# One selector per step: a single VectorE instruction behind each sum, in place of masks and selectors in batches of four

## The reference, cut to what matters

```
def _rel_graph_conv(h, src, dst, etypes, norm, basis, comp, bias, loop_w, apply_relu):   # L0, twice, 4 bases
    hb = jnp.einsum('nd,bdo->bno', h, basis)
    coef = comp[etypes]
    m = coef[:, 0, None] * hb[0][src]
    ...                                                      # the other bases
    m = m * norm[:, None]
    agg = jax.ops.segment_sum(m, dst, num_segments=n)
    out = agg + bias + h @ loop_w
...
    weight = jnp.einsum('rb,bio->rio', w_comp, bases)        # L1: 32 relations, 8 bases
    h_rel = jnp.einsum('ni,rio->rno', x, weight)
    out = jax.ops.segment_sum(h_rel[etype, src] * norm, dst, num_segments=n_nodes)
```

## Time and profile before

| | before |
|---|---|
| median of three runs | 3198.17 us |
| profiled execution | 3180.53 us, span 3179.2 us |
| busy: PE, DVE, ACT, POOL | 3042.3, 2097.8, 1382.1, 1161.1 us |
| L988, sums into G | x664, 454.8 us busy, 685 ns mean, idle before it 154.3 us |
| L864, products with the selector | x1328 matmuls, 659.7 us busy |
| stages with `aggregate` | L0a 42 to 350 us, L0b 532 to 795 us, L1 937 to 1232 us |

### The profile page before, as it was taken

How to read it: one execution, slowest core, us unless ns; L and a number is a source line. 1 busy time by engine, 2 the same in 40 slices (tenths; PEclk the granted TensorE clock), 3 DMA queues, 4 the chain that set the end, 5 groups by cost and what they waited for, 6 DMA issues and landing times.

```text
span 3179.2 us, 44609 instructions
## 1 busy us (share of the span) xinstructions
PE 3042.3 (96%) x14954; PEld 2194.2 (69%) x14954; DVE 2097.8 (66%) x4794; ACT 1382.1 (43%) x2130; POOL 1161.1 (37%) x938
## 2 busy tenths in 40 slices
PE   7999998999979999999999999999999999999999
PEld 3334676444753346876448998789988899879987
DVE  7999423787348864254367678667776777767777
ACT  7999632001340023342254555345543555435554
POOL 4555336556356643431204022511125111441023
PEclk9999998999989999999999999999999999999999
DMA  3555433556236643324103011220014001130012
GB/s 95 149 145 149 165 103 113 162 164 176 79 103 176 170 138 101 97 68 143 33 30 106 8 37 50 66 70 14 31 50 125 18 8 64 43 103 14 8 64 79
DMA packets 125748, 279.37 MB, mean 88 GB/s; under 512 B 22727, under 2 KB 40455, under 8 KB 124499
## 3 DMA queue, kind: packets, MB, share of 16 engines
q0 software_dynamic: 40320, 132.15, 14.8%
q1 hardware_dynamic: 83762, 141.72, 14.2%
q10 hardware_dynamic: 1440, 2.62, 0.2%
HBM read 227.83 MB, written 27.46 MB: 80 GB/s over the span
## 4 chain that ended last, share of the span: by engine, by line
PE 79%; DVE 12%; issue 3%; DMA 3%; ACT 2%; POOL 1%; DVEq 0%; SPq 0%; POOLq 0%; ACTq 0%
PE bank L152 15%; PE bank L154 15%; PE bank L153 15%; PE bank L864 13%; PE bank L2465 5%; PE bank L875 4%; DVE G L988 4%; PE bank L2129 3%; PE bank L1771 2%; PE bank L839 2%; DVE y_tile L2081 1%; DVE y_tile L2083 1%; DVE x_stats L2064 1%; PE bank L1047 1%; DMA yT_lo<-yT_new_lo 1%
## 5 line engine op out<-in xcount | busy, mean ns | idle before, releaser
L864 PE MATMUL bank<-gathered,selector 128*128 x1328 | 659.7, 612 | 52.5 <-SPq L827 30.2
L988 DVE TENSOR_TENSOR G<-G,bank 128x512 f32 x664 | 454.8, 685 | 154.3 <-PE bank L864 102.3
L864 PEld LDWEIGHTS bank<-gathered,selector 128*128 128x128 f32 x1328 | 219.2, 191 | 326.3 <-issue 301.4
L2553 ACT CAST probT<-bank 128x512 fp32r<-128x512 f32 (+2 forms) x480 | 212.1, 516 | 263.8 <-PE bank L2465 262.9
L2635 DVE CUSTOM_DVE_ANT_0 prob<-bank,count_by_src 128x512 f32<-128x512 f32 (+1 forms) x480 | 258.3, 588 | 60.4 <-PE bank L154 60.4
L849 ACT COPY G<-bank 128x512 f32<-128x512 f32 x160 | 81.2, 658 | 497.7 <-PE bank L839 497.7
L1445 POOL TENSOR_TENSOR weight_parts<-weight_ring,weight_parts 128x512 fp32r<-128x512 f32 x130 | 187.3, 1441 | 301.0 <-ACT weight_parts L1378 300.9
L891 ACT ACTIVATE sign_src<-node_iota_16bit,src_float 128x1251 bf16<-128x1251 f16 x208 | 278.6, 1341 | 41.6 <-PE bank L875 19.3
L1404 DVE TENSOR_TENSOR lhs_parts<-G,lhs_parts 128x640 fp32r<-128x640 f32 x122 | 101.5, 832 | 293.9 <-ACT lhs_parts L1376 293.7
L2561 DVE TENSOR_TENSOR probT<-bank,probT 128x512 fp32r<-128x512 f32 (+2 forms) x480 | 254.2, 585 | 51.0 <-ACT probT L2553 50.2
L152 PE MATMUL bank<-weight_parts,lhs_parts 128*128 128x512 f32 x680 | 268.0, 394 | 9.4 <-POOL weight_parts L1445 4.5
(11 more groups left out here) (293 smaller groups left out, 6935.2 us busy)
## 6 DMA issues: line engine op xcount, KB each, us to landing
weight_ring<-in_L_gnn_basis SPq DMA_DIRECT2D x64, 256.0 KB, 2.8
weight_ring<-in_L_gnn_bases SPq DMA_DIRECT2D x64, 256.0 KB, 2.7
x_L<-x_rows SPq DMA_DIRECT2D x50, 256.0 KB, 4.4
x_rows<-x_L SPq DMA_DIRECT2D x50, 256.0 KB, 5.7
yT_hi<-yT_new_hi SPq DMA_DIRECT2D x4, 2560.0 KB, 10.8
yT_lo<-yT_new_lo SPq DMA_DIRECT2D x4, 2560.0 KB
count_rows<-count SPq DMA_DIRECT2D x10, 640.0 KB, 5.9
count_by_dst<-count_rows SPq DMA_DIRECT2D x10, 640.0 KB, 8.3
```

Of the source, the lines that this page charges most:

```text
L864: pe.matmul(bank[s % banks][:], sel[:, s % SELECTORS, :], xs[:, ds(slot[s % BATCH], 1), :].rearrange("p t d -> p (t d)"), start=True, stop ...
L988: dve.tensor_tensor(g, g, bank[s % banks][:], ALU.add).then_inc(*added.inc())
L2553: ins = act.copy(hi, of)
```

## The change

In `aggregate`, the mask tile and the batches go. `select(s)` is one DVE instruction for one step (scalar_tensor_tensor, 128 x 128: grid equals the place, which is a column operand, times coefficient). Eight are made ahead of step 0; after that the selector of step s + 8 is issued right behind the sum of step s, ahead of whatever else that step has for DVE (a count, a one-hot tile, a guest). PE waits for one selector at each step instead of for a batch each four steps.

```
-SELECTORS = 3 * BATCH
+SELECTORS, AHEAD = 3 * BATCH, 2 * BATCH
...
         for s in range(steps):
+            pe.wait_ge(*selected(s + 1))
             if s % BATCH == 0:
                 slot, tiles = (table(C.tile_of_step[path][0:1, s // BATCH, w, :], PE, w, (RING - 1, T)[w])
                                for w in range(2))
-                pe.wait_ge(*selected(s // BATCH + 1))
...
-    def select(i):
-
-        first, n = i * BATCH, min(BATCH, steps - i * BATCH)
-        if first >= SELECTORS:
-            dve.wait_ge(*multiplied(first - SELECTORS + n))
-        if i:
-            dve.wait_ge(*selected(i))
-        dve.tensor_tensor(
-            same[:, 0:n, :],
-            grid.rearrange("p (t n) -> p t n", t=1).to_broadcast([P, n, path.nodes]),
-            C.place[path][:, first:first + n].rearrange("p (t n) -> p t n", n=1).to_broadcast([P, n, path.nodes]),
-            ALU.is_equal).then_inc(*compared.inc())
-        dve.wait_ge(*compared(i + 1))
-        at = first % SELECTORS
-        dve.tensor_tensor(
-            sel[:, at:at + n, :].rearrange("p t (b n) -> p t b n", b=nb),
-            same[:, 0:n, :].rearrange("p t (b n) -> p t b n", b=1).to_broadcast([P, n, nb, path.nodes]),
-            co[:, :, first:first + n].rearrange("p (b n) t -> p t b n", n=1).to_broadcast([P, n, nb, path.nodes]),
-            ALU.mult).then_inc(*selected.inc())
+    def select(s):
+
+        if s >= SELECTORS:
+            dve.wait_ge(*multiplied(s - SELECTORS + 1))
+        dve.scalar_tensor_tensor(
+            sel[:, s % SELECTORS, :].rearrange("p (b n) -> p b n", b=nb),
+            grid.rearrange("p (b n) -> p b n", b=1).to_broadcast([P, nb, path.nodes]), C.place[path][:, s:s + 1],
+            co[:, :, s:s + 1].to_broadcast([P, nb, path.nodes]), ALU.is_equal, ALU.mult).then_inc(*selected.inc())
...
-        select(0)
-        select(1)
+        for s in range(AHEAD):
+            select(s)
...
-                if s // BATCH + 2 < batches:
-                    select(s // BATCH + 2)
...
             dve.tensor_tensor(g, g, bank[s % banks][:], ALU.add).then_inc(*added.inc())
+            if s + AHEAD < steps:
+                select(s + AHEAD)
```

More of the change, by code:

```diff
@@ L332, in prepare @@
     C.after_G = M.at
-    M.at += 4 * (RING * D + SELECTORS * P + BATCH * PATH0.nodes)
+    M.at += 4 * (RING * D + SELECTORS * P)
     C.counting = CountBuffers(C)
@@ L766, in aggregate @@
     if counting:
-        grid, same = C.iota[:, 0:path.nodes], M.new("same_node", [P, BATCH, path.nodes])
+        grid = C.iota[:, 0:path.nodes]
     else:
         grid = bank[3][:, 0:path.nodes]
-        same = bank[3][:, P:P + BATCH * path.nodes].rearrange("p (t n) -> p t n", t=BATCH)
     gathered = [C.landed(f"gathered{u}") for u in range(RING)]
@@ L773, in aggregate @@
     place_free = C.event("gathered_free")
-    compared, selected = C.event("selector_compared"), C.event("selected")
+    selected = C.event("selected")
     added = C.event("added")
@@ L778, in aggregate @@
     turned, taken = C.event("G_turned"), C.event("G_taken")
-    batches = -(-steps // BATCH)
     per = P // path.nodes
```

## The result

The kernel after takes **3233.9 us** (median of 4 runs, 3230.7 to 3235.1), the kernel before 3199.0 (4 runs, 3192.6 to 3200.8): ratio 1.0111, interval 1.0098 to 1.0123, 35 us slower. The forecast was 3202, in a range of 3182 to 3226.

The account below looks back on a forecast made before the run. Waits were taken to decide: L0a's loop through DVE's count, sums in L1, PE and DVE alternating in L0b. +38 - 24 - 10.5 = +3.5, called +4, on 3198.2 gave 3202 us, range 3182 to 3226.

Parts of the forecast that it names:

- L0a, +38: L0a: three selectors per group of four steps stand inside the loop through DVE's third count, 49 groups: +38 us (29 to 50).
- L1, -24: L1, steps 3 to 179: selectors vanish in DVE's idle time between sums, 0.897 us a step instead of 1.04: -24 us.
- L0b, -10.5: L0b: no batch between sums, though guests find the idle time taken: -10.5 us (-4 to -14).
- PE (0.858) and POOL stay under that: L1: PE's step and POOL's gather (1.26 us against 1.32 a tile) fit the new pace; 1.5 us given back.
- Rival A: L0b and L1: gathers set the pace once a tile takes over 1.32 us, half of both gains lost: 3219 us; chance 0.15.
- Rival B: All three stages: small DVE instructions don't overlap, so L1 gains 2, L0b nothing, L0a pays 50: 3246 us; chance 0.06.
- Rival C: L0a: the loop doesn't close through the count, so the three selectors are free: -34.5, 3164 us; chance 0.13.
- The base: Whole kernel: the profiled 3180.5 us lies 0.55% under the runs' median; the same +4 us was carried over to 3198.2.

Follow-up runs that it names:

- the second profile: The kernel before, unchanged, profiled again on chip 7: 3200.5 us, where its first profiled execution took 3180.5.

## Why the prediction was wrong

- **L0a, +38:** right. Loop, place, price (0.26) and number of selectors held; a group took 6.58 for a forecast of 6.57, the stage grew by 41 us, and the term alone cost 40.8. Outside the loop the same instructions leave the kernel at the time of the one before (3205.5 beside 3205.8), with some 4 us left in the stage.
- **L1, -24, and L0b, -10.5:** the failed step is "PE (0.858) and POOL stay under that", for which I gave back 1.5 us. It looked at the work of both engines and put the wait for PE's counts at nothing. Pace and place held to the hundredth. But on chips with late counts (the runs of the result took as long as those do, and the kernel after has the same ten pauses again on chip 14) a pace under some 1.05 us a step isn't let through while POOL gathers: by the profiles 2.8 us in L1 and 3.3 in L0b came of 34.5, by the ratios above 3 to 4 together. 41 - 6 = 35, the measured loss.
- **What was right in it:** with no late counts (plain loads on both sides) the two terms come out at 28.1 and 10.5. The arithmetic of DVE stood; the wrong part was to take the waits that the earlier trace rows show as the only ones there are. Those rows could not show this one: they come from an execution in which no count is late. In the second profile, with late counts, the kernel before is at 187.7 / 176 = 1.07 a step, as the kernel after is (1.07), so the step's new price of 0.90 found nothing to gain.
- **Rival A** named the gathers and gave 3219. The bound is tied to them, but not as it said: hardly a tile was late, L862 waited for one for 0.3 us in 155 (the waits of L1), and POOL itself stood 35.5 us for counts of PE:

```profile
POOL gathered L792 <- PE bank L862: 35.5, 35, 2.6
...
DVE G L973 <- PE bank L862: 17.8, 20, 1.9
...
PE bank L862 <- SPq L825: 0.3, 1, 0.3
```

- **Rival B** is out: the selector starts 0.09 before the sum's row ends, the next instruction 0.08 to 0.09 before the selector's row ends, and with plain loads it vanishes in the gap (169 sums in 155 us). **Rival C** is out: L0a grew by the three selectors.
- **The base:** I saw that the profiled execution lay 18 us under the median and carried the difference over as a constant. It lay in L0b and L1, 10 and 8 us, the very stages whose slack I counted on. Its stages (265.2 and 287.3) are those of chip 3 (265.7 and 286.7), so the profile most likely came from a chip that shows no pauses, and the times from one that does.

What stays open is what makes a count late. Shown: the late counts of L0b and L1 go when plain loads of as many bytes stand in place of the gathers, on a chip that has them; they don't depend on bytes (half of each gather leaves eleven pauses) or on the number of selector counts, or much on PE's load; they differ between chips; and it is PE's counts that are held, several at once, not its multiplications and not DVE's counts. Not shown: which part of a gather does it, its indirect form, POOL's longer work for it or its scattered addresses, since the plain loads changed all three; and whether the recording itself has a part in it. Every time on record comes with a span and a granted clock of the same execution, so no run here shows the kernel unrecorded.

## What to carry to other kernels

Before a freed gap is booked as gain, ask what the profile can't show because the present bound hides it, and test that with an edit that removes the present bound cheaply. A timing from one chip need not hold on the next. When a profile's own time differs from the median, find the stage in which it differs first, for that stage's slack is what a forecast rests on. A small instruction is free or costs its full 0.26 us by its place in the loop that closes last; count the loop's instructions, not the engine's share.

## What the runs showed of the hardware

- The same kernel takes 3182 us on one chip and 3198 to 3206 on three others, and 17.6 of the 20 us between two profiles lie in L0b and L1. L0a gathers as well, a tile in some 1.8 us at its slower steps, and is as long on both kinds of chip (301.8 and 300.8 us).
- Late counts of PE come in rows: three within 0.10 to 0.14 us at five pauses of the kernel after in L1, where a product takes 0.858, and up to 2.4 us behind the last end before them. With plain loads, and in every kernel on chip 3, each recorded count of L1 comes 0.013 to 0.016 us behind its product's end.
- Where counts come late the trace also lacks some of them: of the 248 counts of products in L1 it holds 183 in the kernel after, 187 in the second profile of before, and all 248 in the first profile and in every kernel on chip 3; with plain loads on chip 7, 247 (but 189 of 208 in its L0a, which still gathers).
- The Trainium skill (NOTIFIC — the notification-queue block, "Overflow: three behaviours, one of which stalls the engine") says that the block that writes such records holds its producers back rather than lose one inside. That would join the two observations; no run here tests it, and the missing records speak as much for a loss. DVE's counts miss from the trace too (155 of 248 are there) and none of them is late.
- The granted clock of L1 averaged 0.96 in 155 us of the kernel after and 1.00 with plain loads. The first pauses of L1 in the kernel after, windows of 4 us (columns as above):

```profile
1004.00:1008.00 4.00, 1.28 (x4) 0.45 (x4) 0.95 (x2) 4.00 (x1) 2.36 (x3) 1.00 0.69 201
1008.00:1012.00 4.00, 2.25 (x4) 0.91 (x5) 2.21 (x5) 2.95 (x1) 1.72 (x3) 0.76 0.31 99
1012.00:1016.00 4.00, 4.00 (x5) 1.43 (x5) 2.44 (x6) 0.00 (x0) 1.43 (x2) 0.50 0.47 131
```

PE was busy for 1.28 of 4 us at full clock (2.4 GHz), and the clock then fell to 0.50 (1.2 GHz): five matmuls filled 4 us. In steps 3 to 179 the clock is at 0.50 four times, 17 us in all, each time behind one of the longer pauses, and four sums follow the one before at 1.71 us, two slow matmuls. So a long pause costs a second time, in slow products behind it.
